# Attention outputs turned by ordinary matmuls with only the used columns of the identity

## The chip, the cores and the metric

The kernel runs on one core of one Trainium2 chip. The metric is the device time of one execution in microseconds (us). PE is TensorE, DVE is VectorE, ACT is ScalarE, POOL is GpSimd and SP is SyncE, which issues the transfers.

## The reference

Input `x` is 16 blocks (batch entries) of 128 tokens by 256 channels. Two layers are computed, each sublayer on a layer norm of `x` and added to it: a causal self-attention of 16 heads of 16 with ternary weights and 8-bit activations, a WKV recurrence, and a gated ternary feed-forward; then a self-attention of 32 heads of 8 with rotary positions (8 key heads), a cross-attention of 32 heads of 8 over windows of the context and of `x`, and a feed-forward with a router over six low-rank experts. The part that matters here is the end of each attention:

```python
out = jnp.einsum('bhst,bhtd->bhsd', attn, v)          # 16 heads of 16, or 32 heads of 8
out = out.transpose(0, 2, 1, 3).reshape(B, S, E)      # back to tokens by channels
return _bitlinear(out, w_o)                           # or out @ Wo
```

## The kernel before

The kernel is one program in six stages: setup, `l0` (first self-attention), `mix` (recurrence and feed-forward), `l1a` (second self-attention), `l1x` (cross-attention) and `moe` (experts). Each stage loops over the 16 blocks of 128 tokens, and its work is cut into named pieces. Each engine has one in-order queue. The table `ORDERS` gives for each stage and engine the order of the pieces and by how many blocks each runs ahead or behind, and the tables `TIMES` and `PACE` give each piece a planned time; `merge` interleaves the stages' pieces by these times. The order is thus fixed when the program is built; at run time the engines wait only on semaphores. Successive stages overlap at their ends.

In each attention stage, piece `S` computes scores into PSUM banks, and DVE takes their maxima (`l_neg_max`, `l1a_neg_max` at L881, `l1x_neg_max` at L1155). Piece `M` transposes the maxima and sends them by DMA into the stack of queries. `ST` computes the scores the other way round with the maxima inside, and ACT takes the exps (L648, L930, L1210). `PV` multiplies the values, each with a column of ones appended, by the exps: in bank 7 this gives the raw outputs turned, with 32 rows for a head (or head group), of which the first D are the outputs and the next one is the sum of the exps. D is 16 in `l0` and 8 in `l1a` and `l1x`; the other rows are padding. ACT copies the bank to `oT_raw` (piece `OE`), 128 rows by 512 columns of fp32.

Then comes piece `T1` on PE, which the change touches: four transposes of 128x128 fp32 each turn one quarter of `oT_raw` into bank 0 (`b_tail`). There is one `T1` for a block in `l0` (L733) and there are two in `l1a` (L1006) and in `l1x` (L1332). DVE takes the reciprocal of the sums (piece `T1` of DVE, L579, L885, L1158), multiplies the outputs by it (`T1b`, L583, L891, L1164), and PE transposes the result again (`T4`) and multiplies it by the output weights (`T5`), both into bank 0. `T1` of PE waits for ACT's copy, for DVE to have read the previous half, and for the block before to have left bank 0. The columns of the turned bank come in groups of 32, and DVE reads the first D + 1 of each group.

In the moe stage L1825 and L1828 are ordinary fp32 matmuls (118 and 256 columns, two written of each in a block), and L1839 is one of 256 columns. L952 transposes the normalised input in `l1a`. L296 is in the setup: one fp32 matmul of four columns.

Of the kernel before, what the change touches and what calls it, by code (L numbers as in the profile page):

```python
# [30 lines left out]
P = 128  # L31
# [11 lines left out]
def wait(eng, sem, value):  # L43

    if value > 0:
        eng.wait_ge(sem, value)
# [391 lines left out]
def l0_stage(nc, net, dram, prev, arena):  # L438
# [13 lines left out]
    X, D, NH, NC_, MROW = net.X, 16, 16, 4, 64  # L452
    banks = net.banks
    b_tail, b_qk, b_xv, b_s, b_st, b_ot = banks[0], banks[1], banks[2], banks[3:5], banks[5:7], banks[7]
# [11 lines left out]
    ots = sb("oT_raw", [P, 512])  # L466
# [55 lines left out]
    def dve_program(dve):  # L522
# [10 lines left out]
        for at, piece, c, b, bp in pieces("l0", "dve", NB):  # L533
            yield at
            xb = X[:, b * C:(b + 1) * C]
            tail = b_tail[:].rearrange("p (r g e) -> p (r g) e", r=4, g=4)
            if piece == "F1":
                if b % 4 == 0:
                    dve.wait_ge(net.s_x[b // 4], 16)
                wait(dve, s_f1, 3 * b)  # L540
                dve.bn_stats(stats[:], xb).then_inc(s_f1, 1)
            elif piece == "F1b":
                wait(dve, s_nb, 2 * (b - 1))
                wait_apart(dve, s_f1, b * 3 + 1, net.dve_idle[:])
                dve.bn_aggr(mv[:, bp, :], stats[:]).then_inc(s_f1, 1)
            elif piece == "F1c":
                dve.wait_ge(s_f1, b * 3 + 2)
                dve.tensor_scalar(ve[:, bp, :], mv[:, bp, 1:2], LN_EPS, None, ALU.add).then_inc(s_f1, 1)  # L548
            elif piece == "F3b":
                dve.wait_ge(s_xn, b + 1)  # L550
                wait(dve, s_sc, b - 1)
                quant_scale(0, xn[:, bp, :], amax[:, bp, :]).then_inc(s_f3, 1)
            elif piece in ("F3c", "F3d"):
                step = ("F3b", "F3c", "F3d").index(piece)
                dve.wait_ge(s_f3, b * 3 + step)
                quant_scale(step, xn[:, bp, :], amax[:, bp, :]).then_inc(s_f3, 1)
            elif piece == "F8s":
                if b == 0:
                    dve.wait_ge(prev.s_dve, 15)
                dve.wait_ge(s_f3, b * 3 + 2)  # L560
                wait(dve, s_lo, 2 * (b - 1))
                dve.tensor_scalar(sc[:, bp, :], net.gain_l0[:, 0:3], amax[:, bp, 1:2], None, ALU.mult).then_inc(s_sc, 1)
            elif piece == "F8b":
                dve.wait_ge(s_hi, 2 * (b + 1))
                slots = (q_slots, k_slots)[c][bp]
                src = b_qk[:, 256 * c:256 * c + 256].rearrange("p (h d) -> p h d", d=D)
                dve.scalar_tensor_tensor(out=slots[:, :, 2 - c, :], in0=src, scalar=sc[:, bp, c:c + 1],
                                         in1=slots[:, :, 0, :], op0=ALU.mult, op1=ALU.subtract).then_inc(s_lo, 1)
            elif piece == "S":
                if b == 0 and c == 0:  # L570
                    dve.wait_ge(prev.s_zero, prev.zeroed)
                if c == 0:
                    wait(dve, s_mtp, b)
                dve.wait_ge(s_s, b * NC_ + c + 1)
                dve.tensor_reduce(mm[:, 4 * c:4 * c + 4], b_s[c % 2][:].rearrange("p (h k) -> p h k", k=P),  # L575
                                  AX.X, ALU.max, negate=True).then_inc(s_max, 1)
            elif piece == "T1":
                dve.wait_ge(s_t1, b + 1)
                dve.reciprocal(rden[:], tail[:, :, D]).then_inc(s_t3, 1)  # L579
            elif piece == "T1b":  # L580
                dve.wait_ge(s_t3, b * 5 + 1)
                wait(dve, s_to, b)
                dve.tensor_tensor(o[:].rearrange("p (y d) -> p y d", d=D), tail[:, :, 0:D],  # L583
                                  rden[:].unsqueeze(2).to_broadcast([P, NH, D]), ALU.mult).then_inc(s_t2, 1)
            elif piece == "T3":
                dve.wait_ge(s_t2, b + 1)
                quant_scale(0, o[:], omax[:]).then_inc(s_t3, 1)
            elif piece in ("T3b", "T3c"):
                step = ("T3", "T3b", "T3c").index(piece)
                dve.wait_ge(s_t3, b * 5 + step + 1)  # L590
                quant_scale(step, o[:], omax[:]).then_inc(s_t3, 1)
            elif piece == "T3s":
                dve.wait_ge(s_t3, b * 5 + 4)
                dve.tensor_scalar(so[:, bp:bp + 1], net.gain_l0[:, 3:4], omax[:, 1:2], None, ALU.mult).then_inc(s_t3, 1)
            elif piece == "T5":
                dve.wait_ge(s_t3, b * 5 + 5)
                dve.wait_ge(s_y, b + 1)
                dve.scalar_tensor_tensor(out=xb, in0=b_tail[:, 256:512], scalar=so[:, bp:bp + 1], in1=xb,
                                         op0=ALU.mult, op1=ALU.add).then_inc(s_x, 1)
# [67 lines left out]
    def pe_program(pe):  # L667
        yield opening("l0")

        for at, piece, c, b, bp in pieces("l0", "pe", NB):  # L670
# [33 lines left out]
            elif piece == "M":  # L704
                pe.wait_ge(s_max, (b + 1) * NC_)
                pe.transpose(b_s[0][:, 0:64].bitcast(F16), mm[:], net.ident16[:]).then_inc(s_mtp, 1)
            elif piece == "ST":
                if c == 0:
                    pe.wait_ge(s_md, 16 * (b + 1))
                wait(pe, s_exp, b * NC_ + c - 1)  # L710
                ps = b_st[c % 2]
                pe.matmul(ps[:], net.identb[:], net.cmask[:, 1, :], start=True, stop=False, skip_group_check=True)  # L712
                for x in range(4):
                    h = 4 * c + x
                    ins = pe.matmul(ps[:, P * x:P * x + P], kt[:, b % 3, h, :], qt[:, b % 3, h, :],  # L715
                                    start=False, stop=x == 3, skip_group_check=True)
                ins.then_inc(s_st, 1)
            elif piece == "PV":
                pe.wait_ge(s_v, b + 1)
                pe.wait_ge(s_exp, (b + 1) * NC_)  # L720
                wait(pe, s_oe, b)
                for x in range(4):
                    for y in range(4):
                        ins = pe.matmul(b_ot[32 * y:32 * y + 32, P * x:P * x + P], vs[:, b % 3, 4 * x + y, :],
                                        prob[:, 4 * bp + x, P * y:P * y + P], start=True, stop=True)
                ins.then_inc(s_pv, 1)
            elif piece == "T1":
                if b == 0:
                    take(pe, prev.left, 0)
                pe.wait_ge(s_oe, b + 1)  # L730
                wait(pe, s_x, b)
                for r in range(4):
                    ins = pe.transpose(b_tail[:, P * r:P * r + P], ots[:, P * r:P * r + P], net.ident[:])  # L733
                ins.then_inc(s_t1, 1)
            elif piece == "T4":
                pe.wait_ge(s_oq, b + 1)
                pe.wait_ge(s_t2, b + 1)
                for a in range(2):
                    ins = pe.transpose(b_tail[:, 64 * a:64 * a + 64].bitcast(F16), oq[:, P * a:P * a + P], net.ident16[:])
                ins.then_inc(s_t4, 1)  # L740
            elif piece == "T5":
                pe.wait_ge(s_ot, b + 1)
                for a in range(2):
                    ins = pe.matmul(b_tail[:, 256:512], ot[:, a, :], net.w_l0[:, a, 768:1024], start=a == 0, stop=a == 1)
                ins.then_inc(s_y, 1)
# [9 lines left out]
def l1a_stage(nc, net, dram, prev, before, arena):  # L755
# [98 lines left out]
    def dve_program(dve):  # L854
# [3 lines left out]
        for at, piece, c, b, bp in pieces("l1a", "dve", NB):  # L858
            yield at
            xb = X[:, b * C:(b + 1) * C]  # L860
            tail = b_tail[:].rearrange("p (r g e) -> p (r g) e", r=4, g=4)
            if piece == "F1":
                dve.wait_ge(prev.s_x, b // 2 + 1)
                wait(dve, s_f1, 2 * b)
# [76 lines left out]
    def pe_program(pe):  # L941
        yield opening("l1a")

        for at, piece, c, b, bp in pieces("l1a", "pe", NB):
# [53 lines left out]
            elif piece == "T1":  # L998
# [3 lines left out]
                    take(pe, prev.left, 0)  # L1002
                if c == 0:
                    wait(pe, s_x, b)
                for r in range(4):
                    ins = pe.transpose(b_tail[:, P * r:P * r + P], ots[:, 2 * bp + c, P * r:P * r + P], net.ident[:])  # L1006
                ins.then_inc(s_t1, 1)
            elif piece == "T4":
                pe.wait_ge(s_t2, 4 * (b + 1))
# [17 lines left out]
def l1x_stage(nc, net, dram, prev, before, arena):  # L1027
# [94 lines left out]
    def dve_program(dve):  # L1122
# [3 lines left out]
        for at, piece, c, b, bp in pieces("l1x", "dve", NB):  # L1126
            yield at
            xb = X[:, b * C:(b + 1) * C]
            tail = b_tail[:].rearrange("p (r g e) -> p (r g) e", r=4, g=4)
            if piece == "F1":  # L1130
                dve.wait_ge(prev.s_x, b + 1)
                wait(dve, s_f1, 3 * b)
# [88 lines left out]
    def pe_program(pe):  # L1221
# [3 lines left out]
        for at, piece, c, b, bp in pieces("l1x", "pe", NB):  # L1225
# [98 lines left out]
            elif piece == "T1":  # L1324
# [3 lines left out]
                    take(pe, prev.left, 0)  # L1328
                if c == 0:
                    wait(pe, s_x, b)  # L1330
                for r in range(4):
                    ins = pe.transpose(b_tail[:, P * r:P * r + P], ots[:, 2 * bp + c, P * r:P * r + P], net.ident[:])  # L1332
                ins.then_inc(s_t1, 1)
            elif piece == "T4":
                pe.wait_ge(s_t2, 4 * (b + 1))
# [691 lines left out]
```

## Time and profile before

| | us |
|---|---|
| three runs | 815.83, 820.05, 820.11 |
| median | 820.05 |
| the profiled execution | 819.26 |
| its span, first to last instruction | 817.3 |
| mean granted clock of PE | 0.943 of full speed |

The profile is of one execution. PE has two records for a matmul: the load of the stationary block (PEld, LDWEIGHTS) and the matmul itself (PE, MATMUL). The label names both operands, and the shapes are those of the moving operand. Matmuls are pipelined and their ends are modelled, so the distance from start to start is what one of them costs when they follow each other. The timeline merges instructions of one line that follow each other: start, time from the first's start to the last's end, and their count.

### The profile page before, as it was taken

The page shows a single profiled execution, that of the slowest core. Times are in us where ns is not written, and L with a number is a line of the kernel's source. Part 1 is how long each engine was busy: PE and PEld are TensorE (multiplying, and loading weights), DVE is VectorE, ACT ScalarE, POOL GpSimd, SP SyncE. Part 2 cuts the span into 40 slices and gives each one's busy share as a digit, 9 for nine tenths or more (in the row PEclk, how much of TensorE's full clock was granted, in tenths as well). Part 3 has the DMA queues.
Part 4 walks back from the last instruction along what each step waited for, and adds up shares of the span by engine and source line. Part 5 has one row for each costly group of instructions (what it writes and reads, how often), then busy time and mean ns, then how long its engine had stood idle before and what let it go on. Part 6 is the DMA issues. An engine that isn't in the chain of part 4 may idle for free. (4 is left out here: it accounts for less than half of the span.)

```text
span 817.3 us, 19059 instructions
## 1 busy us (share of the span) xinstructions
PE 661.6 (81%) x6724; PEld 391.7 (48%) x6724; DVE 567.4 (69%) x1616; ACT 504.6 (62%) x1213; POOL 303.7 (37%) x493
## 2 busy tenths in 40 slices
PE   0378888856567778889999877999999999988985
PEld 0145555544345556644544344554454544544553
DVE  6467787878999996677887737555555555557786
ACT  2457778866677655478788762556565665565431
POOL 5212444474677875955655212112111121101110
PEclk9988999977587899999999999999999999999999
DMA  3798986640030000353464423322342224220001
GB/s 117 167 193 169 182 143 121 118 91 11 17 142 14 1 2 1 68 96 67 71 95 67 73 53 72 68 47 48 67 68 51 47 50 79 52 41 2 34 32 40
DMA packets 176238, 58.76 MB, mean 72 GB/s; under 512 B 164560, under 2 KB 174224, under 8 KB 175888
## 3 DMA queue, kind: packets, MB, share of 16 engines
q1 hardware_dynamic: 176144, 57.55, 36.1%
q8 instruction: 54, 0.88, 0.4%
q14 instruction: 40, 0.33, 0.1%
HBM read 15.25 MB, written 2.10 MB: 21 GB/s over the span
## 5 line engine op out<-in xcount | busy, mean ns | idle before, releaser
L1155 DVE TENSOR_REDUCE l1x_neg_max<-bank 128x2 f16<-128x448 f32 (+1 forms) x192 | 117.7, 636 | 99.7 <-PE bank L1273 99.5
L1210 ACT ACTIVATE l1x_probs<-bank 128x512 f32<-128x512 f32 x192 | 106.2, 596 | 46.0 <-PE bank L1294 29.7
L881 DVE TENSOR_REDUCE l1a_neg_max<-bank 128x4 f16<-128x512 f32 x128 | 83.3, 684 | 29.1 <-PE bank L970 28.1
L930 ACT ACTIVATE l1a_probs<-bank 128x512 f32<-128x512 f32 x128 | 69.5, 595 | 30.6 <-PE bank L984 29.8
L1108 POOL TENSOR_TENSOR l1x_rstd<-l1x_var_eps,minus_half 128x1 f32<-128x1 f32 x16 | 8.8, 548 | 206.7 <-DVE l1x_var_eps L1139 206.7
L1648 PE MATMUL bank<-mix_xT_parts,w_ternary 128*128 128x256 f16 x384 | 58.3, 313 | 8.6 <-DVE mix_hidden L1542 8.6
L1648 PEld LDWEIGHTS bank<-mix_xT_parts,w_ternary 128*128 128x128 f16 x384 | 41.2, 112 | 23.2 <-DVE mix_hidden L1542 10.1
L648 ACT ACTIVATE l_probs<-bank 128x512 f32<-128x512 f32 x64 | 36.8, 594 | 22.1 <-PE bank L715 21.5
L575 DVE TENSOR_REDUCE l_neg_max<-bank 128x4 f16<-128x512 f32 x64 | 41.0, 676 | 8.5 <-PE bank L701 8.2
L698 PE MATMUL bank<-causal_masks,ident_bf 128*128 128x512 bf16 x64 | 28.2, 441 | 22.3 <-DMA l_kT<-k_stack 21.6
L1471 POOL TENSOR_TENSOR mix_hidden_parts<-mix_hidden,mix_hidden_parts 128x256 f16<-128x256 f32 x48 | 35.6, 748 | 21.2 <-ACT mix_hidden_parts L1600 21.2
L512 POOL TENSOR_TENSOR l_rstd<-l_var_eps,minus_half 128x1 f32<-128x1 f32 x16 | 8.9, 556 | 83.1 <-DVE l_var_eps L548 83.1
L1600 ACT CAST mix_hidden_parts<-mix_hidden 128x256 f16<-128x256 f32 x48 | 19.3, 403 | 29.7 <-DVE mix_hidden L1542 29.3
L1273 PE MATMUL bank<-l1x_kT,l1x_qT 64*64 64x224 f16 (+1 forms) x1024 | 35.7, 236 | 0.0
L1720 POOL TENSOR_TENSOR moe_rstd<-moe_var_eps,minus_half 128x1 f32<-128x1 f32 x16 | 8.8, 547 | 71.9 <-DVE moe_var_eps L1738 71.9
L995 PE MATMUL bank<-l1a_probs,l1a_v_ones 128*32 128x512 f32 x256 | 34.1, 605 | 0.0
L1316 PE MATMUL bank<-l1x_probs,v_ones 128*32 128x512 f32 x256 | 34.1, 605 | 0.0
L1218 ACT COPY l1x_oT<-bank 128x256 f32<-128x256 f32 x16 | 6.0, 373 | 42.8 <-PE bank L1337 42.8
L712 PE MATMUL bank<-causal_masks,ident_bf 128*128 128x512 bf16 x64 | 28.7, 449 | 4.3 <-DMA l_qT<-l_neg_maxT 4.3
L1273 PEld LDWEIGHTS bank<-l1x_kT,l1x_qT 64*64 64x64 f16 x1024 | 25.9, 107 | 7.8
L1290 PE MATMUL bank<-ident_repeated,window_of_keys 64*128 64x256 bf16 x256 | 25.1, 274 | 5.1 <-ACT l1x_probs L1210 3.1
L970 PE MATMUL bank<-l1a_kT,l1a_qT 64*128 64x128 f16 x512 | 25.3, 218 | 4.3 <-DVE l1a_neg_max L881 4.3
(271 smaller groups left out, 1907.8 us busy)
## 6 DMA issues: line engine op xcount, KB each, us to landing
x_residual<-x_in SPq DMA_DIRECT2D x4, 512.0 KB, 4.9
mix_ctx_in<-ctx_in SPq DMA_DIRECT2D x16, 128.0 KB, 2.1
l1x_ctx_in<-ctx_in SPq DMA_DIRECT2D x16, 128.0 KB, 2.1
out_dram<-moe_out SPq DMA_DIRECT2D x16, 128.0 KB, 1.7
w_f<-w_in SPq DMA_DIRECT2D x2, 704.0 KB, 6.2
w_attn_f<-w_l_in SPq DMA_DIRECT2D x1, 1024.0 KB, 6.1
q_stack<-q_begin_in SPq DMA_DIRECT2D x1, 1024.0 KB, 5.1
l1x_qT<-l1x_neg_maxT SPq DMA_DIRECT2D x64, 2.0 KB
```

The source lines that it names most:

```text
L575: dve.tensor_reduce(mm[:, 4 * c:4 * c + 4], b_s[c % 2][:].rearrange("p (h k) -> p h k", k=P), AX.X, ALU.max, negate=True).then_inc(s_max, 1)
L648: act.activation(prob[:, 4 * bp + c, :], b_st[c % 2][:], ACT.Exp).then_inc(s_exp, 1)
L712: pe.matmul(ps[:], net.identb[:], net.cmask[:, 1, :], start=True, stop=False, skip_group_check=True)
L881: dve.tensor_reduce(mm[:, 16 * j + 4 * s:16 * j + 4 * s + 4], b_s[c % 3][:].rearrange("p (r k) -> p r k", k=P), AX.X, ALU.max, negate=True ...
L930: act.activation(prob[:, c, :], b_st[c % 2][:], ACT.Exp).then_inc(s_exp, 1)
L995: ins = pe.matmul(b_ot[32 * x:32 * x + 32, :], vs[:, b % 3, 4 * c + x, 0:32], prob[:, 4 * c + x, :], start=True, stop=True)
L1155: dve.tensor_reduce(mm[:, first:first + count], scores, AX.X, ALU.max, negate=True).then_inc(s_max, 1)
L1210: act.activation(prob[:, c, :], b_st[c % 2][:], ACT.Exp).then_inc(s_exp, 1)
L1273: ins = pe.matmul(ps[:, n * x:n * x + n], qt[rows, b % 3, 4 * s + 2 * r2 + u, 64 * z:64 * z + 64], keys, start=False, stop=True, skip_grou ...
L1316: pe.matmul(b_ot[32 * x:32 * x + 32, :], vs[:, b % 3, 4 * c + x, 0:32], prob[:, 6 * c + x, :], start=True, stop=False, skip_group_check=True)
L1471: pool.tensor_tensor(hp[:, ip, 1, m, :], hf[:, m % 2, :], hp[:, ip, 0, m, :], ALU.subtract).then_inc(s_hl, 1)
L1648: ins = pe.matmul(b_h[m % 3][:, W * v:W * v + W], net.w12[:, k % 2, v, P * m:P * m + P], xp[:, ip, k // 2, k % 2, :], start=k == 0, stop=k ...
```

## The change

In the three attention stages each of the four transposes of `T1` becomes an ordinary matmul. The stationary operand is the same quarter of `oT_raw`. The moving operand is no longer the whole identity but the first D + 1 columns of each group of 32: 4 x 17 = 68 columns in `l0` and 4 x 9 = 36 in `l1a` and `l1x`. The results stand packed in bank 0 (272 or 144 columns instead of 512), and DVE's view of it follows. Semaphores, waits and orders stay.

```diff
@@ l0, dve
-            tail = b_tail[:].rearrange("p (r g e) -> p (r g) e", r=4, g=4)
+            tail = b_tail[:, 0:272].rearrange("p (r g e) -> p (r g) e", r=4, g=4)
@@ l0, pe, piece T1
+                used = net.ident[:].rearrange("p (g e) -> p g e", g=4)[:, :, 0:D + 1]
                 for r in range(4):
-                    ins = pe.transpose(b_tail[:, P * r:P * r + P], ots[:, P * r:P * r + P], net.ident[:])
+                    ins = pe.matmul(b_tail[:, 68 * r:68 * r + 68], ots[:, P * r:P * r + P], used, start=True, stop=True)
                 ins.then_inc(s_t1, 1)
@@ l1a and l1x, dve
-            tail = b_tail[:].rearrange("p (r g e) -> p (r g) e", r=4, g=4)
+            tail = b_tail[:, 0:144].rearrange("p (r g e) -> p (r g) e", r=4, g=4)
@@ l1a and l1x, pe, piece T1
+                used = net.ident[:].rearrange("p (g e) -> p g e", g=4)[:, :, 0:D + 1]
                 for r in range(4):
-                    ins = pe.transpose(b_tail[:, P * r:P * r + P], ots[:, 2 * bp + c, P * r:P * r + P], net.ident[:])
+                    ins = pe.matmul(b_tail[:, 36 * r:36 * r + 36], ots[:, 2 * bp + c, P * r:P * r + P], used, start=True, stop=True)
                 ins.then_inc(s_t1, 1)
```

## Rows read from the trace of the kernel before

**Rows 1.** The page's busy times, and one of its costliest groups.

```profile
PE 661.6 (81%) x6724; PEld 391.7 (48%) x6724; DVE 567.4 (69%) x1616; ACT 504.6 (62%) x1213; POOL 303.7 (37%) x493
...
L1210 ACT ACTIVATE l1x_probs<-bank 128x512 f32<-128x512 f32 x192 | 106.2, 596 | 46.0 <-PE bank L1294 29.7
```

**Rows 2.** Windows: stretch, length; busy time of each engine; clock; DMA share; GB/s.

```profile
60.00:120.00 60.00, 48.91 (x552) 33.70 (x551) 46.78 (x138) 45.23 (x100) 21.45 (x31) 0.89 0.86 166
...
370.00:450.00 80.00, 80.00 (x723) 39.79 (x715) 62.49 (x157) 65.33 (x150) 45.84 (x73) 1.00 0.48 76
450.00:520.00 70.00, 57.54 (x624) 30.61 (x619) 41.41 (x102) 37.92 (x88) 12.29 (x22) 1.00 0.36 64
520.00:700.00 180.00, 168.50 (x2146) 89.08 (x2145) 95.50 (x237) 106.34 (x234) 26.18 (x43) 1.00 0.32 58
```

**Rows 3.** Waits of PE, 540 to 700 us: total, times, longest.

```profile
PE bank L1299 <- ACT l1x_probs L1210: 5.6, 9, 0.6
```

**Rows 4.** Waits of PE, 60 to 180 us.

```profile
PE bank L698 <- DMA l_kT<-k_stack: 12.1, 6, 2.9
...
PE bank L712 <- DMA l_qT<-l_neg_maxT: 4.1, 4, 1.8
```

**Rows 5.** The chain that ended last: start, length, what.

```profile
755.23 0.59 PE bank L1332 x4
755.81 0.44 PE bank L1825 x4
756.25 0.87 PE bank L1828 x4
```

**Rows 6.** Timeline of the second self-attention stage, PE.

```profile
398.84 0.63 PE L1006 MATMUL bank<-ident,l1a_oT_raw 128*128 128x128 f32 x4
...
399.41 0.40 PE L970 MATMUL bank<-l1a_kT,l1a_qT 64*128 64x128 f16 x8
...
407.44 0.41 PE L1006 MATMUL bank<-ident,l1a_oT_raw 128*128 128x128 f32 x2
```

**Rows 7.** Timeline of the cross-attention stage, PE and DVE.

```profile
572.91 0.66 PE L1332 MATMUL bank<-ident,l1x_oT_raw 128*128 128x128 f32 x4
...
579.23 0.26 DVE L1158 RECIPROCAL l1x_rden<-bank 128x16 f32<-128x16 f32 x1 [1.56 <-PE bank L1332]
...
580.16 1.14 DVE L1155 TENSOR_REDUCE l1x_neg_max<-bank 128x2 f16<-128x448 f32 x2
...
582.84 0.38 PE L1266 MATMUL bank<-window_end,ident_bf 64*64 64x448 bf16 x4
...
589.43 0.44 PE L1332 MATMUL bank<-ident,l1x_oT_raw 128*128 128x128 f32 x2
```

**Rows 8.** Groups by line, whole run: loads; busy, mean ns; idle before.

```profile
L1006 PEld LDWEIGHTS bank<-ident,l1a_oT_raw 128*128 128x128 f32 x128 | 13.7, 141 | 15.8 <-issue 14.6
...
L1825 PEld LDWEIGHTS bank<-w_moe,moe_xT 128*128 128x128 f32 x64 | 8.3, 190 | 11.3 <-ACT moe_xT L1797 6.7 <-issue 4.7
```

**Rows 9.** Timeline of the first attention stage, PE.

```profile
110.88 0.39 PE L715 MATMUL bank<-l_qT,l_kT 128*128 128x128 f16 x4
...
111.10 0.61 PE L733 MATMUL bank<-ident,l_oT_raw 128*128 128x128 f32 x4
...
111.54 0.38 PE L698 MATMUL bank<-causal_masks,ident_bf 128*128 128x512 bf16 x1
...
117.79 0.39 PE L712 MATMUL bank<-causal_masks,ident_bf 128*128 128x512 bf16 x1 [1.32 <-DMA l_qT<-l_neg_maxT]
...
183.75 1.06 PE L733 MATMUL bank<-ident,l_oT_raw 128*128 128x128 f32 x4
```

**Rows 10.** Timeline of setup, second self-attention and moe stages, PE and loads.

```profile
10.63 0.59 PE L296 MATMUL bank<-abs_sums,ones 128*128 128x4 f32 x2 [10.63 <-DVE abs_sums L245]
...
441.50 0.20 PEld L952 LDWEIGHTS bank<-ident,l1a_xn 128*128 128x128 f32 x2
...
757.59 0.30 PEld L1839 LDWEIGHTS bank<-b_moe,moe_low_rankT 128*128 128x128 f32 x2 [0.38 <-ACT moe_low_rankT L1804]
```

## What was predicted

> **What bounds the kernel now.** I read the page's busy times first [rows 1]: PE 661.6 of 817.3 us, DVE 567.4, ACT 504.6. The ends of matmuls are modelled, so a high PE share proves little; I went on to the windows by stage, then to the waits. By windows [rows 2] PE is busy 80.00 of 80 us in the second self-attention stage (370 to 450) and 168.50 of 180 in cross-attention (520 to 700), both at full clock, and 48.91 of 60 in the first attention stage. In cross-attention its largest wait is for ACT's exps, 5.6 us over 9 blocks, 0.6 a block [rows 3], and ACT at that line idles 29.7 us for PE's scores over the run [rows 1]: each waits for the other in turn, with PE setting the turn. From 60 to 180 us, about 12 blocks, PE waits 16.2 us for two kinds of DMA [rows 4]. The chain of the last stretch is PE after PE and runs through one of the changed groups, L1332 [rows 5]. The pace is strict: the first group of a block comes at 398.84 and again at 407.44, 8.60 us [rows 6]; in cross-attention at 572.91 and 589.43, 16.52 us [rows 7]. So in the second and third attention stages time put on PE is time of the kernel.
>
> **What the change is, instruction by instruction.** It touches groups of four transposes: one group in each of 16 blocks of the first stage, two a block in each of the others, 80 groups. An fp32 transpose is one load and one matmul: the trace has 128 loads at L1006 for 32 groups of four. An ordinary fp32 matmul is two of each: the moe stage writes two at L1825 in each of 16 blocks, 32, and the trace has 64 loads [rows 8]. So each group goes from 4 loads and 4 matmuls of 128 columns to 8 loads of the full 128x128 block and 8 matmuls of 36 columns (68 in the first stage). Columns fall from 512 to 288, or rise to 544; the stationary side, which the diff does not shrink, doubles in count.
>
> **Price of a group now.** From its first matmul to the next piece's, 398.84 to 399.41, it is 0.57 where its first load hides in part, and 0.59 in the chain at 755.23 [rows 5, 6]. Its four members stand 0.11 apart, 0.44 in all, which is the whole price at 111.10 (to 111.54), where the next piece uses all 128 rows [rows 9]. The other 0.15 is the first load, 0.05, and about 0.10 of turning to 64-row work. At the half clock of 1.2 GHz the same four take 1.06 to their end instead of 0.61 (183.75 [rows 9]).
>
> **Price of a group after.** Does a 36-column matmul pass at the pace of its columns or of its load? The nearest rows are an ordinary fp32 matmul with a full stationary block and few columns, L1825 with 118: four take 0.44, 0.11 each. L1828, with 256 columns, takes 0.87 for four, 0.22 each [rows 5], so 0.85 ns a column and 0.100 for 118 columns: the spacing is a little above that, and the load tells why. The two loads of L1839 last 0.30 together with nothing before them; one lasts 0.19 by L1825's mean [rows 8, 10], so they start 0.11 apart. The two loads of L952's transposes last 0.20 [rows 10] at 0.14 each (L1006's mean [rows 8]): 0.06 apart. An ordinary fp32 load thus holds the loader for 0.11, a transpose's for half of that. 36 columns (0.03 of streaming) hide under it, and so do 68 (0.06). After: 8 x 0.11 = 0.88, the last stream 0.03 and the turn 0.10, less some 0.04 of the first load behind the work before: 0.97. I take **+0.38 us** a group at 36 columns. In the first stage 0.88 + 0.06, less 0.04, is 0.90 against 0.44: +0.46, and +0.9 at half clock, which I put at 3 of the 16 groups. Bounds from both sides: if loads went as those of a full fp16 block, whose matmuls at L715 stand (111.10 - 110.88) / 4 = 0.055 apart [rows 9], a group would take 8 x 0.055 + 0.15 = 0.59, +0. The upper bound is L296, one written matmul of four columns, again two in the trace, on a PE idle for 10.63 us before: they take 0.59 together [rows 10], at most 0.3 each, so 2.4 + 0.1, +1.9 a group. I take L1825, which has the same block and an engine in full flow.
>
> The Trainium skill, Perfetto Trace Analysis, section "Transposes", says to do a logical transpose in transpose mode and not as a standard matmul. It gives no price; the trace agrees by the loads above. The Trainium skill, TensorE: Matmul & The Clock Gate, section "LDWEIGHTS (loading the stationary operand)", puts a load at its columns over 1.2 GHz, 107 ns for 128, whatever the mode; the trace agrees for an ordinary fp32 load (0.11) and not for a transpose's (0.06). By the page the old group's first load costs 0.05 more, so the growth would be +0.33 instead of +0.38: about +25 us instead of +28.
>
> **Rest of the edits.** DVE reads the same 16 x 9 (16 x 17) numbers from PSUM at another stride; the reciprocal is 0.26 us now [rows 7]; bound -0.05 to +0.05, I take 0, since count and dtype stay. The strided identity costs 0 (bound: to +0.05 a member, as large as the room under a load; none seen). No wait is added, but one ends later: DVE's reciprocal waits for the group, 1.56 us at 579.23, and behind it in DVE's queue stand the maxima that free the score banks for PE. Those run until 580.16 + 1.14 = 581.30, and PE's next scores start at 582.84 [rows 7]: 0.4 later still holds, with 1.1 left. ACT's next copy of raw outputs waits for the group two blocks back, far off.
>
> **The sum.** PE in all: 32 x 0.38 = 12.2, twice; 13 x 0.46 + 3 x 0.9 = 8.7; 33 us. On the path: of the second stage's 32 groups some 6 lie in the handover (450 to 520: PE busy 57.54 of 70 [rows 2]) and count half, 29 x 0.38 = 11.0. Of the third's 32 I count 30, 11.4: the last overlap the moe stage, but the chain runs through one there [rows 5]. In the first stage PE has waits to lose, 16.2 / 12 = 1.3 us a block against +0.5. Yet one of them hangs on PE: the maxima go PE, ACT, DMA and back to PE (1.32 us of wait at 117.79 [rows 9]), and the group stands in that loop, ahead of the block's last scores. I take 60%, 5.2. Together **+27.6 us**: span 817.3 + 27.6 = 844.9. The profiled execution took 819.26 with its 817.3 of span, 1.96 around it, and is 0.8 under the median of 820.05; so 846.9 on its own scale, 847 as forecast.
>
> **Rivals.**
> *Slack takes half.* The first stage's waits swallow all 8.7 us, and the 0.6 a block for ACT [rows 3] shrinks by a half: 22.4 less 5 is 17, time 836; with the wait gone whole, 22.4 - 9 = 13, time 832. Against: ACT idles for PE as well [rows 1].
> *No change.* The loads go at fp16's 0.055, the lower bound: +0, 819. Against: L1825's spacing, and L1839's loads.
> *Faster.* The second instruction of a pair finds the block in the array and needs no load, so columns decide: 8 x 0.03 + 0.15 = 0.39 against 0.59, -0.2 x 64 = -13, the first stage even (8 x 0.06 = 0.48 against 0.44): 807. It decides below a spacing of 0.055. For it: fewer columns. Against: 64 loads in the trace for 32 written matmuls [rows 8].
> *More than the load.* All 33 on the path, and DVE's later maxima cost PE 0.25 in each of 32 blocks: 33 + 8 = 41, time 860. Against: the 1.1 us left at DVE.
> That the diff makes something else than ordinary fp32 matmuls of 36 and 68 columns I see no ground for.
>
> **Chances.** Forecast (837 to 856) 0.74; half taken (825 to 837) 0.10; more than the load 0.05; no change 0.05; faster 0.06. Within 0.5%, 816 to 824, a measurement of this kernel can't tell from no change. So slower 0.89, same 0.05, faster 0.06. The range holds the forecast's spread and most of the half case: 832 to 857.
>
> **What would show it.** L1006 and L1332 with 256 loads and 256 matmuls of 128x36, L733 with 128 of 128x68, loads near 190 ns and not 140. A group in the second stage spans 0.95 to 1.0 us with members 0.11 apart. The periods go from 8.60 to about 9.36 and from 16.52 to about 17.3, PE's waits for ACT in cross-attention stay near 0.6 a block, the clock stays full there. I am wrong if members stand under 0.08 apart, or if the periods grow by under 0.5 us though the group grows: then there was slack that these views hide.

## The result, and the profile after

The changed kernel took 850.26 us (median of 4 runs, 842.4 to 857.84) against 818.1 (4 runs, 815.83 to 820.11): ratio 1.036, 95% interval 1.028 to 1.044, slower. Five further rounds gave 849.35 against 819.05, ratio 1.034 (1.030 to 1.038). The forecast was 847 in a range of 832 to 857. The profiled execution of the changed kernel was a slow one (857.84 us, mean granted clock 0.935 against 0.945 to 0.957 in the other three), which the ratio leaves out; the rows below are therefore of the profiled execution of the repetition, 845.3 us with a span of 843.4.

Groups by line of the changed kernel, loads and matmuls of the turned outputs (busy us, mean ns | idle before). They answer to [rows 8].

```profile
L1008 PEld LDWEIGHTS bank<-ident,l1a_oT_raw 128*128 128x128 f32 x256 | 32.0, 196 | 15.7 <-issue 14.6
L1335 PEld LDWEIGHTS bank<-ident,l1x_oT_raw 128*128 128x128 f32 x256 | 31.2, 191 | 5.8 <-issue 5.6
L734 PEld LDWEIGHTS bank<-ident,l_oT_raw 128*128 128x128 f32 x128 | 18.3, 220 | 2.8 <-issue 2.8
...
L1335 PE MATMUL bank<-ident,l1x_oT_raw 128*128 128x36 f32 x256 | 34.3, 280 | 0.0
```

The matmuls of the same line in the kernel before:

```profile
L1332 PE MATMUL bank<-ident,l1x_oT_raw 128*128 128x128 f32 x128 | 20.8, 285 | 0.0
```

In the second and third stage the loads doubled, from 128 to 256, and each lasts 191 to 196 ns instead of 140 or 141. Each matmul has 36 columns where it had 128, and yet the line keeps PE busy for 34.3 us instead of 20.8.

The timeline of the changed kernel's second self-attention stage, PE, beside [rows 6] (start, time to the last one's end, count):

```profile
405.98 1.08 PE L1008 MATMUL bank<-ident,l1a_oT_raw 128*128 128x36 f32 x8
407.00 0.40 PE L971 MATMUL bank<-l1a_kT,l1a_qT 64*128 64x128 f16 x8
...
412.89 1.05 PE L1008 MATMUL bank<-ident,l1a_oT_raw 128*128 128x36 f32 x8
413.88 0.40 PE L971 MATMUL bank<-l1a_kT,l1a_qT 64*128 64x128 f16 x8
```

The two groups of a block hold PE for 0.99 (412.89 to 413.88, where it was 0.57) and 1.02 us (405.98 to 407.00). Within a group, (1.08 - 0.28) / 7 = 0.11 lies between members (0.28 is the record of one matmul). The period is 9.44 us where it was 8.60 [rows 6].

The cross-attention stage, PE, of the changed kernel, beside [rows 7]:

```profile
593.01 1.08 PE L1335 MATMUL bank<-ident,l1x_oT_raw 128*128 128x36 f32 x8
594.02 0.38 PE L1268 MATMUL bank<-window_end,ident_bf 64*64 64x448 bf16 x4
594.24 0.36 PE L1275 MATMUL bank<-l1x_kT,l1x_qT 64*64 64x224 f16 x8
594.53 0.39 PE L1292 MATMUL bank<-ident_repeated,window_of_keys 64*128 64x256 bf16 x4
...
609.60 0.39 PE L1301 MATMUL bank<-ident_repeated,window_of_keys 64*128 64x512 bf16 x2 [0.62 <-ACT l1x_probs L1212]
...
610.14 1.08 PE L1335 MATMUL bank<-ident,l1x_oT_raw 128*128 128x36 f32 x8
```

and the same stretch of the kernel before:

```profile
573.71 0.36 PE L1273 MATMUL bank<-l1x_kT,l1x_qT 64*64 64x224 f16 x8
574.25 0.40 PE L1290 MATMUL bank<-ident_repeated,window_of_keys 64*128 64x256 bf16 x4 [0.18 <-ACT l1x_probs L1210]
```

The period goes from 16.52 to 610.14 - 593.01 = 17.13, +0.61, though two groups grew by 1.01 - 0.59 = 0.42 each. The second pair of fences shows where the rest went. Before, PE came from the scores at 573.71 to L1290 only 0.54 later, after a wait for ACT's exps; after, the same step takes 0.29 (594.24 to 594.53) and no wait is left. The longer group, just ahead, gave ACT the time. The other wait for ACT, 0.62 at L1301, stays.

The windows of the changed kernel, beside [rows 2] (stretch, length, busy time of PE, PEld, DVE, ACT, POOL, clock, DMA share, GB/s):

```profile
370.00:450.00 80.00, 80.00 (x713) 44.97 (x714) 58.14 (x149) 60.17 (x137) 42.21 (x68) 1.00 0.41 68
450.00:540.00 90.00, 78.14 (x774) 45.91 (x774) 48.26 (x116) 45.53 (x105) 18.54 (x31) 0.94 0.31 57
540.00:720.00 180.00, 171.69 (x2189) 97.59 (x2183) 93.53 (x232) 105.12 (x231) 24.67 (x41) 1.00 0.34 58
```

PE stays full while DVE and ACT thin out (DVE 62.49 to 58.14 of 80): they wait for PE. The clock holds inside the stages; in the handover it was 0.94 in this execution.

By the first and last group of each stage, the span's +26.1 us (843.4 - 817.3) are: 1.4 up to the second stage's first group (365.8 against 364.4), 13.8 across that stage's groups (159.8 against 146.0), 3.3 in the handover (16.1 against 12.8), 7.5 across the third stage's (272.6 against 265.1), 0.1 behind. The 1.4 says little of the first stage: that point came at 376.5 in the changed kernel's first profile and at 373.4 in only_l0 below, so the first stage moves by several us from one execution to the next. Its cost is read from the times of only_l0.

### The profile page after: what moved, and what is told of

Read it like the earlier page. It is cut to its first block and busy times, and to the rows that moved or that the text cites. A ratio compares the mean times of both kernels' runs of the same rounds, so it can differ in the third digit from the quotient of the medians.

```text
span 855.9 us, 19681 instructions
## 1 busy us (share of the span) xinstructions
PE 699.3 (82%) x7026; PEld 439.1 (51%) x7044; DVE 569.9 (67%) x1616; ACT 504.5 (59%) x1213; POOL 303.8 (35%) x493
## 5 line engine op out<-in xcount | busy, mean ns | idle before, releaser
L1651 PE MATMUL bank<-mix_xT_parts,w_ternary 128*128 128x256 f16 x384 | 55.7, 302 | 10.5 <-DVE mix_hidden L1545 10.5
L1008 PEld LDWEIGHTS bank<-ident,l1a_oT_raw 128*128 128x128 f32 x256 | 32.7, 200 | 15.5 <-issue 14.3
L701 PE MATMUL bank<-l_kT,l_qT 128*128 128x128 f16 x256 | 28.5, 241 | 10.8 <-DMA l_kT<-k_stack 9.0
L1008 PE MATMUL bank<-ident,l1a_oT_raw 128*128 128x36 f32 x256 | 35.4, 286 | 1.6 <-DVE x_residual L896 1.5
L712 PE MATMUL bank<-causal_masks,ident_bf 128*128 128x512 bf16 x61 | 27.9, 458 | 9.1 <-DMA l_qT<-l_neg_maxT 9.1
L1335 PE MATMUL bank<-ident,l1x_oT_raw 128*128 128x36 f32 x256 | 34.3, 280 | 0.0
L1335 PEld LDWEIGHTS bank<-ident,l1x_oT_raw 128*128 128x128 f32 x256 | 31.2, 191 | 5.8 <-issue 5.6
```

Of the source, the lines that this page charges most:

```text
L1008: ins = pe.matmul(b_tail[:, 36 * r:36 * r + 36], ots[:, 2 * bp + c, P * r:P * r + P], used, start=True, stop=True)
L1335: ins = pe.matmul(b_tail[:, 36 * r:36 * r + 36], ots[:, 2 * bp + c, P * r:P * r + P], used, start=True, stop=True)
L1651: ins = pe.matmul(b_h[m % 3][:, W * v:W * v + W], net.w12[:, k % 2, v, P * m:P * m + P], xp[:, ip, k // 2, k % 2, :], start=k == 0, stop=k ...
```

## The experiments

There are eleven runs, on three chips; each ratio is to the kernel before on the same chip. A cost in us is the ratio less one, times the median of the kernel before (819.05 for the first four runs), and its interval is that of the ratio. The repetition's expectation:

> The changed kernel once more, for its trace where the clock holds between the second and the third attention stage. Load theory (each ordinary fp32 matmul waits for a 0.11 us load, and there are twice as many): 842 to 852 us, members of a group 0.112 apart, periods 9.44 and 17.13 again, about 0.84 and 0.60 above before; of the 33 us over before some 12 stand in the second, some 9 in the third stage and the rest in the first stage and the handovers. Clock theory (much of the loss is a half clock between the stages, brought about by the change): in the executions with the clock at full there, the loss falls under 22 us.

Measured: 849.35 us, group members 0.112 apart, periods 9.44 and 17.13. The clock theory falls with two figures. By span and mean granted clock (full or half), the 23 executions of the kernel before spent a median of 94.8 us at half clock, and the six of the changed kernel 91.6: the change brought none. And the half clock about the handover comes and goes between profiles: none in all_columns below, which loses 35 us of span, 13.7 us of it in only_l1a, 7 to 10 us in three kernels that are faster than before (half_used, half_turned and tiles4). What the half clock does explain is the spread within one kernel: over those 23 executions each us of it goes with 0.40 us of time (correlation 0.93).

**One stage at a time.** `only_l0`, `only_l1a` and `only_l1x` take the change's hunks of one stage each, for instance:

```diff
 l1a_stage, pe, piece T1 (l0 and l1x as before)
-                    ins = pe.transpose(b_tail[:, P * r:P * r + P], ots[:, 2 * bp + c, P * r:P * r + P], net.ident[:])
+                    ins = pe.matmul(b_tail[:, 36 * r:36 * r + 36], ots[:, 2 * bp + c, P * r:P * r + P], used, start=True, stop=True)
```

> The change in the first attention stage alone. Load theory: 16 groups grow by 0.46 to 0.5, 8.7 us on PE, of which PE's waits for DMA hide some: +5 us over before (2 to 10). Rival (that stage is bound by DMA, the added PE time is hidden): under +2 us.

Measured: 827.33 us, ratio 1.007 (1.004 to 1.011), +6.1 us. The groups grew as said: in the timeline of only_l0, 0.90 from 112.86 to 113.76, where it was 0.44 [rows 9].

```profile
112.86 1.06 PE L734 MATMUL bank<-ident,l_oT_raw 128*128 128x68 f32 x8
113.76 0.38 PE L698 MATMUL bank<-causal_masks,ident_bf 128*128 128x512 bf16 x1
```

The 16 groups took 17.4 us instead of 9.4, so 8.0 were added and 6.1 show, with an interval of 3.4 to 8.7. That DMA waits hid the small difference fits, but is not shown.

> The change in the second self-attention stage alone. Load theory: 32 groups by 0.42, nothing hides it in the steady part, half of it in the handover: period 8.60 to 9.44, +12 us (10 to 15). Rival (slack in the stage): the group grows and the period by less than 0.6, under +8 us.

Measured: 834.75 us, ratio 1.017 (1.012 to 1.021), +13.8 us; period 9.44. The growth in the steady part (0.84 a block over 13 blocks) explains 11; the rest is in the last blocks and the handover, with 13.7 us at half clock in this profile.

> The change in the cross-attention stage alone. Load theory: 32 groups by 0.43, less 0.25 a block, a wait for ACT's exps that the longer group covers: period 16.53 to 17.13, +9 us (7 to 12). Rival (PE time counts whole): period +0.85, +13 us.

Measured: 829.15 us, ratio 1.011 (1.008 to 1.014), +8.9 us; period 17.13. The three sum to 28.8 us; the whole change costs 0.0343 x 819.05 = 28.1. By differences of medians it is 34.1 against 30.3, so the agreement is good to some 4 us. Within that, the costs add up and none of the stages hides another's.

**Load or columns.** `all_columns` is the change with the whole identity as moving operand:

```diff
-                    ins = pe.matmul(b_tail[:, 36 * r:36 * r + 36], ots[:, 2 * bp + c, P * r:P * r + P], used, start=True, stop=True)
+                    ins = pe.matmul(b_tail[:, P * r:P * r + P], ots[:, 2 * bp + c, P * r:P * r + P], net.ident[:], start=True, stop=True)
```

> Ordinary matmuls as in the change, but with all 128 columns of the identity, and DVE reads the turned bank at the old stride of 32. Load theory: a member still costs 0.11, since 128 columns stream in 0.107 beside a load of as much; only the last stream of a group is 0.08 longer: 2 to 6 us over the changed kernel, 847 to 857. Column theory (what a member costs goes by its columns, and the loss has another cause, such as the strides of the identity or of DVE): 0.107 against 0.03 a member, 8 members, 64 groups: 35 us and more over the changed kernel.

Measured: 852.46 us, ratio 1.035 (1.030 to 1.041). Cross-attention, PE, of all_columns:

```profile
582.95 1.16 PE L1332 MATMUL bank<-ident,l1x_oT_raw 128*128 128x128 f32 x8
584.04 0.38 PE L1266 MATMUL bank<-window_end,ident_bf 64*64 64x448 bf16 x4
```

A group is 1.09 against 1.01: 3.5 times the columns cost one longer last stream, 0.08, and members stand 0.112 apart as with 36. The column theory, and with it any cause in the strides, falls. The columns that the change saved were worth one stream of 0.08 a group and nothing between the members: the periods of all_columns are 9.59 and 17.28, 0.15 above the change's, which makes 5 us over the 16 blocks of the two stages.

**PE time alone.** `twice` does the old four transposes two times over:

```diff
-                for r in range(4):
+                for r in (0, 1, 2, 3, 0, 1, 2, 3):
                     ins = pe.transpose(b_tail[:, P * r:P * r + P], ots[:, 2 * bp + c, P * r:P * r + P], net.ident[:])
```

> The kernel before with each group's four transposes done twice over, which adds 4 x 0.109 = 0.44 us of PE to a group and nothing else of the change. If PE time at this place is what the change costs: period +0.87 in the second stage and +0.6 in the third, as in the change, 843 to 855 us in all. Rival (the loss comes from what ordinary matmuls do besides, to the clock or to DVE's reads): the time stays 10 us or more away from that of the changed kernel.

Measured: 848.23 us, ratio 1.032 (1.027 to 1.037); periods 9.46 and 17.15; a group 1.02 (580.39 to 581.41 in its timeline). With nothing of the change but its PE time, the loss is the change's within the intervals. That answers for DVE's packed reads as well, of which `twice` has none.

**The load made cheap, at fp16.** `half_used` is the change with `oT_raw` and the identity in fp16; `half_turned` is the kernel before with both in fp16 and the turned bank in fp16. Both round the raw outputs to fp16.

```diff
-    prob, ots = sb("probs", [P, 8, 512]), sb("oT_raw", [P, 4, 512])
+    prob, ots = sb("probs", [P, 8, 512]), sb("oT_raw", [P, 4, 512], F16)
-                used = net.ident[:].rearrange("p (g e) -> p g e", g=4)[:, :, 0:D + 1]
+                used = net.ident16[:].rearrange("p (g e) -> p g e", g=4)[:, :, 0:D + 1]
```

> The changed kernel with ACT's copy of the raw outputs in fp16 and the fp16 identity, so that an ordinary matmul is one load and one matmul again; the outputs are rounded to fp16 there. Load theory: members 0.055 apart (the fp16 load), a group 4 x 0.055 + 0.13 = 0.35 against 0.59 before, 0.24 x 64 = 15 us less, some 2 more from the first stage, less what waits swallow: 800 to 810 us. Rival (an ordinary matmul with few columns costs a fixed amount above 0.1 whatever its type): no faster than before, 817 or more.

> As half_used, but with fp16 transposes of all 128 columns into fp16, the old form of the group. Load theory: 128 columns of fp16 stream in 0.053, as long as the load of 0.055, so the columns are worth nothing: within 3 us of half_used. Column theory: 36 columns in place of 128 are worth 0.04 a member, 0.16 a group, 10 us, so it is about 10 us slower than half_used.

Measured: half_used 806.28 us, ratio 0.980 (0.976 to 0.985); half_turned 811.66, ratio 0.987 (0.981 to 0.993). The second self-attention stage, PE: first half_used, then half_turned.

```profile
403.33 0.27 PE L1008 MATMUL bank<-ident_f,l1a_oT_raw 128*128 128x36 f16 x4
403.62 0.40 PE L971 MATMUL bank<-l1a_kT,l1a_qT 64*128 64x128 f16 x8
```

```profile
407.70 0.40 PE L1006 MATMUL bank<-ident_f,l1a_oT_raw 128*128 128x128 f16 x4
408.03 0.40 PE L970 MATMUL bank<-l1a_kT,l1a_qT 64*128 64x128 f16 x8
```

Four members of 36 columns end after 0.27, with 0.18 for the last: about 0.03 apart (0.025 in the records). With 128 columns they stand 0.055 apart. So the spacing was wrong in both expectations: the load of a full fp16 block is not 0.055 but 0.025 or less, and the columns do count once the load is that short. The time of half_used lies in its range of 800 to 810 all the same, and that is luck in part, as the next fence shows. The medians of the two differ by 5.4 us, between the 3 of one theory and the 10 of the other; the intervals of the two ratios overlap, and the periods (8.30 and 16.14 against 8.34 and 16.27) account for 2.7 us over 16 blocks. The direction of the load theory held and its fp16 price did not. ACT's copy is no rival as a cause of the gain: to fp16 it takes 589 to 600 ns, to fp32 589 to 591.

The cheaper groups pay off only in part. Behind the first group of a block, half_used has a wait that the kernel before does not have (second self-attention stage, PE):

```profile
401.22 0.26 PE L1008 MATMUL bank<-ident_f,l1a_oT_raw 128*128 128x36 f16 x4
401.79 0.40 PE L971 MATMUL bank<-l1a_kT,l1a_qT 64*128 64x128 f16 x8 [0.31 <-DVE l1a_neg_max L882]
```

The next scores wait for DVE to have read the old ones. The period ends at 8.30 in half_used and at 8.34 in half_turned, which has the same wait, up to 0.2 us in 7 blocks; so this stage has about 0.3 us a block to give before DVE's maxima count. tiles4 below ends at 8.31, where its trace lists no such wait; what holds it there is not shown.

**The load made cheap, at fp32.** Each ordinary matmul is cut by its stationary columns into two or four. The parts are written to different partitions of bank 0 (in the expectations' words, they lie in different column tiles of the array). The cut into four is `tiles4`, shown here; `tiles2` has 64 for 32 and 2 for 4, and `tiles4_l1` leaves the first stage as before.

```diff
                 for r in range(4):
-                    ins = pe.matmul(b_tail[:, 36 * r:36 * r + 36], ots[:, 2 * bp + c, P * r:P * r + P], used, start=True, stop=True)
+                    for k in range(4):
+                        ins = pe.matmul(b_tail[32 * k:32 * k + 32, 36 * r:36 * r + 36], ots[:, 2 * bp + c, P * r + 32 * k:P * r + 32 * k + 32], used, start=True, stop=True)
```

> The changed kernel with each ordinary matmul cut in two by its stationary columns (64 tokens each, two column tiles of the array that run beside each other). Same columns streamed by each, same fp32. Load theory: a load is as long as it has stationary columns, 0.055 us for 64, and the two tiles load side by side, so a group is 8 x 0.055 + 0.13 = 0.57, the price of the old group: 815 to 825 us. Rival (a member has a fixed cost above 0.1, whatever its load): twice as many members, at least as slow as the changed kernel, 845 or more.

> As tiles2 with four column tiles of 32 tokens. Load theory: a load of 32 columns is 0.027 and four run side by side, the 36 columns stream in 0.03, so a group is 8 x 0.03 + 0.13 = 0.37 to 0.4 in the second and third stage, 0.2 under before: 64 x 0.2 = 13 us less; in the first stage 8 x 0.057 = 0.46, as before. 803 to 812 us, faster than both kernels at full fp32. Rival: 32 members a group at a fixed cost each (0.025, as half_used showed for its members): 0.8 a group, 835 to 845.

> tiles4 in the second and third attention stages, the old transposes in the first. Load theory: 68 columns twice over are worth as much as 128 once there, so within 3 us of tiles4. Rival: the first stage's 32 short members cost it 0.2 a group or more, and this is 3 us and more faster than tiles4.

Measured: tiles2 818.83 us, ratio 0.999 (0.995 to 1.002); tiles4 813.22, ratio 0.991 (0.988 to 0.994); tiles4_l1 813.75, ratio 0.992 (0.989 to 0.995). Cross-attention, PE: first tiles2, then tiles4.

```profile
590.74 0.66 PE L1338 MATMUL bank<-ident,l1x_oT_raw 128*64 128x36 f32 x16
591.33 0.38 PE L1270 MATMUL bank<-window_end,ident_bf 64*64 64x448 bf16 x4
```

```profile
587.18 0.47 PE L1338 MATMUL bank<-ident,l1x_oT_raw 128*32 128x36 f32 x32
587.58 0.38 PE L1270 MATMUL bank<-window_end,ident_bf 64*64 64x448 bf16 x4
```

The same fp32 numbers, the same 36 columns, two and four times the instructions: the group falls from 1.01 to 0.59 and to 0.40 us as the loads shrink from 128 to 64 and 32 columns. In the second stage tiles4's two groups take 0.54 and 0.42. The loads in both, by line:

```profile
L1338 PEld LDWEIGHTS bank<-ident,l1x_oT_raw 128*64 128x64 f32 x512 | 17.5, 137 | 6.6 <-issue 6.6
```

```profile
L1338 PEld LDWEIGHTS bank<-ident,l1x_oT_raw 128*32 128x32 f32 x1024 | 11.4, 110 | 6.6 <-issue 6.6
```

Mean loads of 191, 137 and 110 ns at 128, 64 and 32 columns: each column more adds 0.84 ns. One after the other, 32 loads of 32 columns would take 32 x 32 x 0.84 = 860 ns by that; the whole group takes 0.40 us, so they run side by side. tiles4 beats both kernels at fp32, the one before by 7.4 us, which is only 0.9% but clear of its interval. In the first stage its group (0.61 at the median) is longer than the transposes' 0.44 to 0.51 and that costs nothing that intervals of about 2.6 us could show: tiles4_l1 is no faster. The expectation of tiles4 said 803 to 812, and 813.2 is 1 us outside. The periods tell why: 16.53 to 16.35 in cross-attention, only half of the 0.38 that two groups gave up: at the step where before waited 0.18 for ACT's exps (L1290, here L1294), tiles4's PE waits 2.6 us for them in 7 blocks, 0.37 each, and 0.4 in two more blocks for the DMA of the maxima.

## Why the prediction was right

*PE sets the pace.* Shown by `twice`: PE time of about the same size at the same place costs 26 us, the change 28. It holds for added time; of time taken away, half_used and tiles4 show that only a part comes back.

*An ordinary fp32 matmul is two loads and two matmuls.* Shown by the counts, 256 for 128.

*A member costs its load, 0.11.* Right: 0.112 in all three stages. Shown from three sides: with 128 columns the spacing stays 0.112, with loads of 64 and 32 columns the group gets cheaper, and with fp16 loads it is cheapest. The Trainium skill, TensorE: Matmul & The Clock Gate, section "LDWEIGHTS (loading the stationary operand)", has the load go by its stationary columns, at 1/1.2 = 0.83 ns each; the trace agrees for an ordinary fp32 load with 0.84 ns a column. The Trainium skill, TensorE: Matmul & The Clock Gate, section "Weight-path perf modes — Fast Weight Load (FWL) and DoubleRow", has a faster load for a full block of a type other than fp32 and gives about 2x as measured, which makes 0.05 us as an estimate; half_used shows 0.025 or less, so the trace agrees that it is faster, and for how much the measurement decides.

*The price of a group.* +0.38 was put where +0.42 was measured (1.01 against 0.59; 0.99 against 0.57): the members stand at 0.112 rather than 0.11, which is 0.016 of a group, and the rest lies in what was put for the last stream, the turn to 64-row work and the hidden part of the first load, which no run separates. Over the 64 groups of the two stages it makes 2.6 us. In the first stage the +0.46 (0.90 against 0.44) was near: 8.0 us over the 16 groups of only_l0, where 8.7 was put.

*What lies on the path.* By stage: 11.0 forecast and 13.8 measured in the second, 11.4 and 8.9 in the third, 5.2 and 6.1 in the first. The sum of 27.6 met 28.1, with errors that offset, so that it came within 0.5 us is luck; the mechanism and the range are not. The periods show the two errors clear of noise: forecast 9.36 and about 17.3, measured 9.44 and 17.13. The second stage was under since the group's price was, and since the handover hid little where I had let it hide half: in all_columns, at full clock there, the stage's last three periods grow by 2.3 us for six groups that grow by 2.8. The third was over: the wait of the rival "slack takes half" does shrink, though not the one I priced. I had looked at the largest, L1299, which stays 0.62; the one that went is at L1290, behind the scores that follow the changed group, listed with 0.18 and worth 0.25 a block in fact (0.54 against 0.29). It swallowed some 4 us (16 x 0.25). In the first stage some 2 of 8 us went.

*No change* and *Faster* fell with the members' spacing; half_used comes out at the 807 of *Faster*, but because its matmuls are single loads of fp16 and short, not because a second instruction needs no load. *More than the load*: DVE's slack of 1.1 us held: its reciprocal waits up to 2.0 us where it was 1.6, and PE has no wait for DVE in that stage from 560 to 720 us.

Open is what sets the half clock in the handover. It appears in some profiles and not in others of like kernels; the 3.3 us that the handover grew in after_again's profile are not parted between it and the longer groups.

## What to carry to other kernels

Before cutting the moving columns of a matmul, ask which side sets its spacing: with a full fp32 stationary block the load does, at 0.11 us, twice per written matmul, and fewer than about 128 columns save no more than the end of the last stream. A transpose of fp32 has one load of half the length and one stream of 0.109 us, so it is the cheaper form for turning 128x128 (all_columns costs 3.5% over it). If few columns are wanted, cut the stationary side too, into parts that go to different partitions and load side by side. Before making one engine faster, look for the wait that comes next: here about half of the PE time saved came back as waits for ACT, or for DVE's maxima. And where a bound is taken from a row (fp16's 0.055), check that the row is bound by the thing it is to price.

## What the runs showed of the hardware that I had not expected

A full 128x128 fp16 block loads in 0.025 us or less: half_used's members are that far apart, where the kernel's other fp16 rows, with 128 columns, show 0.055 and had looked like a load. An fp32 load of the same block costs 0.112, over four times as much for twice the bytes. And 32 small instructions in four column tiles (0.40 us a group in cross-attention) are faster than four transposes (0.59); I expected that only once the loads had been measured.
